# Transposing x and x1 by block flips and on-chip DMAs in a two-layer graph attention kernel

## The reference

```
layer 0:  q, k, v = x Wq', x Wk', x Wv' + bv          (per graph, 12 heads)
          s = q k' / sqrt(384) + (adj + adj);  p = softmax(s), 0 for rows of s that are all 0
          x1 = layernorm(x + (p v) Wo' + bo)
layer 1:  q, k, v = x1 Wq + bq, x1 Wk + bk, x1 Wv + bv
          s = q k' / sqrt(32) + beta adj, masked where adj <= 0;  p = softmax(s)
          out = layernorm(x1 + p v)
```

## Time and profile before

| | |
|---|---|
| time, median of 3 runs | 2354.26 us (2352.67 to 2358.37) |
| the profiled execution | 2356.46 us, span 2354.6 us |
| TensorE busy in matmuls | 2139.2 us, 91% of the span |
| VectorE | 1879.1 us, 80% |
| ScalarE | 1891.4 us, 80% |
| GpSimd | 1555.8 us, 66% |
| DMA engines, share of the span | 48.7%, 299 MB |
| mean granted clock of TensorE | 0.98 of full speed |

### The profile page before, as it was taken

How to read it: one execution, slowest core, us unless ns; L and a number is a source line. 1 busy time by engine, 2 the same in 40 slices (tenths; PEclk the granted TensorE clock), 3 DMA queues, 4 the chain that set the end, 5 groups by cost and what they waited for, 6 DMA issues and landing times.

```text
span 2354.6 us, 86096 instructions
## 1 busy us (share of the span) xinstructions
PE 2139.2 (91%) x23808; PEld 1929.9 (82%) x23808; DVE 1879.1 (80%) x8451; ACT 1891.4 (80%) x7688; POOL 1555.8 (66%) x2188
## 2 busy tenths in 40 slices
PE   5899999999999999999999999999999999999863
PEld 5888888888888888888888888888888888888853
DVE  4588888888888888888888888888888888887763
ACT  5688888888888888888888888888888888887764
POOL 5666666676776676676676676676676676676642
PEclk9999999999999999999999999999999999999975
DMA  5255454454554554554544544545545445444433
GB/s 141 74 135 129 130 139 127 129 140 126 128 140 122 133 138 119 137 135 119 143 129 122 141 129 122 139 129 127 134 129 132 129 129 137 124 130 124 121 100 78
DMA packets 234654, 299.36 MB, mean 127 GB/s; under 512 B 26704, under 2 KB 226384, under 8 KB 234576
## 3 DMA queue, kind: packets, MB, share of 16 engines
q1 hardware_dynamic: 234576, 298.43, 48.7%
HBM read 46.67 MB, written 25.17 MB: 31 GB/s over the span
## 4 chain that ended last, share of the span: by engine, by line
ACT 25%; issue 21%; POOL 21%; PE 15%; DVE 13%; ACTq 2%; POOLq 1%; DVEq 1%; DMA 1%; SPq 0%
ACT prob L586 19%; DVE neg_s L697 6%; POOL flip L914 4%; POOL x_bo L879 4%; PE s_bank L415 4%; PE r_bank L365 3%; PE r_bank L366 3%; PE r_bank L367 3%; POOL adj L903 3%; POOL mask L900 2%; POOL y L924 2%; POOL rstd L863 2%; ACT k0T L547 2%; POOL bias L889 1%; ACT k1T L551 1%
## 5 line engine op out<-in xcount | busy, mean ns | idle before, releaser
L586 ACT ACTIVATE prob<-neg_s,neg_max 128x128 f32<-128x128 f32 x3072 | 1183.3, 390 | 206.8 <-DVE neg_max L697 205.4
L697 DVE CUSTOM_DVE_ANT_0 neg_s<-s_bank,bias 128x128 f32<-128x128 f32 x3072 | 670.3, 286 | 147.8 <-PE s_bank L415 117.5
L586 ACT ACTIVATION_READ_ACCUMULATOR prob<-neg_s,neg_max 128x1 f32 x3072 | 589.6, 192 | 0.0
L932 POOL TENSOR_TENSOR prob<-prob,inv_sum 128x512 f32<-128x512 f32 x384 | 388.9, 1041 | 23.1 <-DVE inv_sum L785 19.8
L365 PE MATMUL r_bank<-x1T_hi,w_hi 128*128 128x256 f32 x1152 | 358.6, 311 | 3.4 <-ACT k0T L547 2.1
L365 PE MATMUL r_bank<-xT_hi,w_hi 128*128 128x256 f32 x1152 | 351.6, 305 | 10.5 <-DVE xT_lo L719 10.5
L914 POOL TENSOR_TENSOR flip<-neg_s 128x768 f32<-128x768 f32 x128 | 234.6, 1833 | 189.1 <-DVE neg_max L697 165.7
L367 PE MATMUL r_bank<-xT_hi,w_lo 128*128 128x256 f32 x1152 | 327.3, 284 | 0.0
L366 PE MATMUL r_bank<-x1T_lo,w_hi 128*128 128x256 f32 x1152 | 326.4, 283 | 0.0
L366 PE MATMUL r_bank<-xT_lo,w_hi 128*128 128x256 f32 x1152 | 326.3, 283 | 0.0
L367 PE MATMUL r_bank<-x1T_hi,w_lo 128*128 128x256 f32 x1152 | 325.4, 282 | 0.0
(11 more groups left out here) (75 smaller groups left out, 5424.2 us busy)
## 6 DMA issues: line engine op xcount, KB each, us to landing
prob0T<-flip SPq DMA_DIRECT2D x512, 192.0 KB, 3.5
prob1T<-stage SPq DMA_DIRECT2D x512, 192.0 KB, 3.7
x_in<-in_x_dram SPq DMA_DIRECT2D x128, 192.0 KB, 3.0
x_late<-x SPq DMA_DIRECT2D x64, 384.0 KB, 2.6
out_dram<-y SPq DMA_DIRECT2D x128, 192.0 KB, 2.3
adj<-in_adj_dram SPq DMA_DIRECT2D x256, 64.0 KB, 2.3
stage<-in_L_gnn_Wv_dram SPq DMA_DIRECT2D x2, 576.0 KB, 5.1
stage<-in_L_gnn_Wq_dram SPq DMA_DIRECT2D x2, 576.0 KB, 5.9
```

The lines of the kernel that those rows point to most:

```text
L586: act.activation(prob[layer][:, h, :], neg_s[layer][:, h, :], ACT.Exp, bias=neg_max[layer][:, h:h + 1], scale=-1.0, accum_out=row_sum[laye ...
L697: dve.tensor_tensor_reduce(neg_s[layer][:, h, :], s_bank[b][:, (h // HC) * N:(h // HC + 1) * N], bias[layer][q.parity][:, g, :], -1.0, BIG ...
L932: pool.tensor_tensor(prob[0][:, hs, :], prob[0][:, hs, :], inv_sum0[:, hs].unsqueeze(2).to_broadcast([P, HC, N]), ALU.mult).then_inc(probn ...
```

## The change

TensorE no longer transposes x and x1. `flip_xT` and `flip_x1T` on VectorE flip the 32x32 blocks of one graph's x or x1 into `flip_x`, `spread_rows` on SP moves the blocks between partitions with four DMAs for both graphs of a pair into `spread_x`, ScalarE copies the high part from there (`high_rows`), and GpSimd takes the low part (`low_rows`). x and x1 share `flip_x` and `spread_x`. The features come out in another order on the partitions, so the weights are loaded with their rows in that order, by three DMAs each.

x of pair n+2 is flipped near the end of body n and spread right behind the layer-0 probabilities of graph 1; its high part is still taken at the same place of the body of n+1. There is one more body at the start. x1 of pair n-1 is flipped in the middle of body n. The first eight users of the old ring (four of them transposes) go to a ring without the transposes; the Q and K product 4 of layer 0 and the scores of layer 1 go ahead of product 0 of layer 1 in TensorE's and ScalarE's queues. x, adj for layer 0 and the biases have one buffer each, so their loads and sums wait for the pair before. The layer-1 bias is made in two halves, and the second half goes to the end of the body.

```diff
-FIRST, LAST = -1, PAIRS + 3
+FIRST, LAST = -2, PAIRS + 3
...
-        x_in = [sb(f"x_in{b}", [P, 2, D]) for b in range(2)]
+        x_in = sb("x_in", [P, 2, D])
...
-        adj0 = [sb(f"adj0_{b}", [P, 2, N]) for b in range(2)]
+        adj0 = sb("adj0", [P, 2, N])
...
-        bias = [[sb(f"bias{l}_{b}", [P, 2, N]) for b in range(2)] for l in range(2)]
+        bias = [sb(f"bias{l}", [P, 2, N]) for l in range(2)]
...
+        flip_x = sb("flip_x", [P, NB, C, 2, HD])
+        spread_x = sb("spread_x", [P, NB, C, 2, HD])
...
+            def spread_rows(flipped, loaded, q):
+
+                if q.valid():
+                    sp.wait_ge(flipped, q.count(1, 1, 1))
+                    for i in range(NB):
+                        sp.dma_start(spread_x[:, i, :, :, :].rearrange("p c g b -> p (c g b)"),
+                                     flip_x[HD * i:HD * (i + 1), :, :, :, :].rearrange("p j c g b -> p (j c g b)")
+                                     ).then_inc(loaded, 16)
+
             def body(r, off):
                 n = Pair(r, off)
+                load_adj1(n.plus(-2))
                 store(n.plus(-4), 1)
                 keep_x1(n.plus(-2))
                 spread_probs(0, n, 0)
+                spread_rows(x1flip_done, x1t_loaded, n.plus(-1))
                 spread_probs(1, n.plus(-3), 1)
-                load_x(n.plus(3))
-                load_adj0(n.plus(3))
-                load_adj1(n.plus(-1))
+                if not is_peeled(r, off, -2):
+                    load_x(n.plus(2))
+                    load_adj0(n.plus(2))
                 store(n.plus(-3), 0)
                 spread_probs(0, n, 1)
+                spread_rows(xflip_done, xt_loaded, n.plus(2))
...
                 spread_probs(1, n.plus(-2), 0)
...
                 scores(0, n, 0, r)
-                transpose_x(nxt, 0, r)
-                transpose_x(nxt, 1, r)
...
-                transpose_x1(prev, 0, r)
-                transpose_x1(prev, 1, r)
...
+            def high_rows(dst, loaded, layer, done, q, g):
+                if q.valid():
+                    act.wait_ge(loaded, q.count(16 * NB // 2, 1, 16 * NB // 2))
+                    if g == 0:
+                        act.wait_ge(g_done[layer], q.count(3, 0, 0))
+                        act.wait_ge(v_done[layer], q.count(1, 0, 0))
+                    act.activation(dst[:, :, g * N:(g + 1) * N].rearrange("p c (i b) -> p c i b", i=NB),
+                                   spread_x[:, :, :, g, :].rearrange("p i c b -> p c i b"), ACT.Copy
+                                   ).then_inc(done, 1)
...
+                exps(0, n, 1, 2, 6)
                 high_x1T(prev, 0)
                 high_x1T(prev, 1)
...
-                exps(0, n, 1, 2, 9)
+                exps(0, n, 1, 6, 9)
...
+            def flip_rows(src, done, q, g):
+                dve.transpose(flip_x[:, :, :, g, :].rearrange("p j c b -> p c j b"),
+                              src.rearrange("p (c j a) -> p c j a", c=C, j=NB)).then_inc(done, 1)
...
                 flip_probs(0, n, 0)
+                attention_out1(prev3, 0)
+                flip_x1T(prev, 0)
                 inverse_sums1(prev3, 1)
                 flip_probs(1, prev3, 1)
-                attention_out1(prev3, 0)
+                flip_x1T(prev, 1)
                 values_out(0, nxt, 0)
...
                 flip_probs(0, n, 1)
+                flip_xT(nxt.plus(1), 0)
+                flip_xT(nxt.plus(1), 1)
+                attention_out1(prev3, 1)
                 inverse_sums1(prev2, 0)
                 flip_probs(1, prev2, 0)
...
+            def low_rows(dst, hi, hi_done, done, q, g):
+                if q.valid():
+                    m = slice(g * N, (g + 1) * N)
+                    pool.wait_ge(hi_done, q.count(1, g, 1))
+                    pool.tensor_tensor(dst[:, :, m].rearrange("p c (i b) -> p c i b", i=NB),
+                                       spread_x[:, :, :, g, :].rearrange("p i c b -> p c i b"),
+                                       hi[:, :, m].bitcast(F32).rearrange("p c (i b) -> p c i b", i=NB), ALU.subtract
+                                       ).then_inc(done, 1)
...
                 fold_scores0(n, 0)
                 inverse_std(1, prev4, 1)
+                low_xT(nxt, 0)
+                low_xT(nxt, 1)
                 normalise0(n, 0)
                 inverse_std(0, prev, 1)
-                make_bias1(prev2)
...
                 residual1(prev3, 0)
-
+                make_bias1(prev2, 0)
                 residual0(nxt, r)
-                make_bias0(nxt)
+
+                make_bias0(nxt, 0)
+                low_x1T(prev, 0)
+                low_x1T(prev, 1)
+                make_bias0(nxt, 1)
                 fold_scores0(n, 1)
                 inverse_std(1, prev3, 0)
                 normalise0(n, 1)
...
+                make_bias1(prev2, 1)
                 residual1(prev3, 1)
```

More of the change, by code:

```diff
@@ L275, in load_weights @@
                     sp.wait_ge(w_lo_done[i - NS], 1)
-                sp.dma_start(w_stage[i % NS], wts[i].rearrange("(c p) o -> p c o", p=P)
-                             ).then_inc(w_loaded[i], 16)
+                for c in range(C):
+                    rows = wts[i][c * P:(c + 1) * P, :]
+                    if i != WO0:
+                        rows = rows.rearrange("(j a) o -> a j o", j=NB)
+                    sp.dma_start(w_stage[i % NS][:, c, :], rows).then_inc(w_loaded[i], 16)
             load_x(Pair(0, 0))
@@ L486, in body @@
                 attend(0, n, 0, r)
+                project_qk(0, nxt, 4, r)
+                scores(1, prev2, 0, r)
                 project_qk(1, prev, 0, r)
-                scores(1, prev2, 0, r)
-                project_qk(0, nxt, 4, r)
                 project_out0(n, 0, r)
@@ L875, in residual0, with make_bias0 @@
                         pool.wait_ge(const_done, 1)
-                    pool.wait_ge(x_loaded[b], q.loads(2))
+                    pool.wait_ge(x_loaded, q.count(16, 1, 16))
                     pool.wait_ge(y0_done, q.plus(-2).count(1, 1, 1))
                     for g in range(2):
-                        pool.tensor_tensor(x_bo[b][:, g, :], x_in[b][:, g, :], bo_row[:], ALU.add
+                        pool.tensor_tensor(x_bo[b][:, g, :], x_in[:, g, :], bo_row[:], ALU.add
                                            ).then_inc(x_bo_done, 1)
-            def make_bias0(q):
+            def make_bias0(q, g):
@@ L884, in make_bias0 @@
                 if q.valid():
-                    b = q.parity
-                    pool.wait_ge(adj0_loaded[b], q.loads(2))
-                    pool.wait_ge(neg_done[0], q.plus(-2).count(H, 1, H))
-                    for g in range(2):
-                        pool.tensor_tensor(bias[0][b][:, g, :], adj0[b][:, g, :], adj0[b][:, g, :], ALU.add
-                                           ).then_inc(bias0_done, 1)
-            def make_bias1(q):
+                    pool.wait_ge(adj0_loaded, q.count(16, 1, 16))
@@ L894, in make_bias1 @@
+                    pool.wait_ge(neg_done[0], q.plus(-1).count(H, g, H))
+                    pool.tensor_tensor(bias[0][:, g, :], adj0[:, g, :], adj0[:, g, :], ALU.add
+                                       ).then_inc(bias0_done, 1)
+            def make_bias1(q, g):
                 if q.valid():
-                    b = q.parity
                     pool.wait_ge(adj1_loaded, q.count(16, 1, 16))
-                    pool.wait_ge(neg_done[1], q.plus(-2).count(H, 1, H))
+                    pool.wait_ge(neg_done[1], q.plus(-1).count(H, g, H))
+                    pool.wait_ge(bias1_steps, q.count(3, g, 0))
@@ L906, in make_bias1 @@
-                    for g in range(2):
-                        pool.tensor_tensor(bias[1][b][:, g, :], adj1[:, g, :], mask1[:, g, :], ALU.add).then_inc(bias1_steps, 1)
+                    pool.tensor_scalar(mask1[:], adj1[:, g, :], 0.0, -MASKED, ALU.is_le, ALU.mult
+                                       ).then_inc(bias1_steps, 1)
+                    pool.tensor_scalar(adj1[:, g, :], adj1[:, g, :], 0.0, beta_col[:], ALU.max, ALU.mult
+                                       ).then_inc(bias1_steps, 1)
@@ new lines, in make_bias1 @@
+                    pool.wait_ge(bias1_steps, q.count(3, g, 2))
+                    pool.tensor_tensor(bias[1][:, g, :], adj1[:, g, :], mask1[:], ALU.add).then_inc(bias1_steps, 1)
+            def low_rows(dst, hi, hi_done, done, q, g):
[6 more added lines that the diff above has]
+                                       ).then_inc(done, 1)
```

136 lines of the change are left out of this document (54 added, 82 removed).

## The result

The changed kernel takes 2746.16 us, median of 4 runs (2741.01 to 2747.39), beside 2354.37 us for the kernel before (median of 4): 1.166 times as long, 95% interval 1.1636 to 1.1678. The forecast was 2736 us. TensorE was rid of its transposes, and the whole got 392 us slower.

What follows compares the result with a forecast made beforehand. The bound was a 35.1 us loop through in-order queues, with TensorE nearly full. Both journeys make it 41.4: 2356.5 + 60 x 6.3 + 4 = 2738.5, less 2 for the median, 2736 us; range 2620 to 2920.

Steps and rivals of the forecast that it cites:

- Both journeys on one loop: The forecast: x's and x1's flip, spread and copies both lengthen the turn, 35.1 to 41.4 us; chance 0.74.
- the four terms: Graph-1 probability flip to exponentials behind x's copies 10.8 us, to normalisation 11.7, to graph-1 fold 10.4, to next flip 8.5.
- if ScalarE does not wait: Stated sign of a wrong prediction; ScalarE was to idle 2.5 to 3 us a turn before x's copies.
- The DMAs: SP's four spreading DMAs, for x and again for x1: 4.8 us from first issue to landing, bounds 4.2 and 6.05.
- The start: Before the first projection x must be flipped and spread, but weights arrive about then: 4 us once.
- a term of 6.3 us a turn: Predicted growth of one turn, 41.4 us against 35.1, charged for 60 turns.
- Single buffers and the bias half at nothing: Later loads of x and adj have over 8 us of cover; the bias half moved to the body's end: no cost.
- Rival, only x1's journey: x's spread lands before ScalarE asks; a loop through x1 and TensorE gives 37.5 us a turn, 2505 us; chance 0.06.
- Rival, the clock falls: TensorE's waits halve its clock once a turn, 1 to 2.5 us on the loop, 2800 to 2890 us; chance 0.10.
- What would show it: Profile signs: turn about 41 us, ScalarE idle before both copies, late fold, TensorE about 76%, first waiting at graph 1's value product.

Runs made afterwards that it cites:

- the two padded kernels: Changed kernel with four tiny DMAs on SP ahead of x's four spreading DMAs, or ahead of x1's: 2906.34 us and 2911.76 us.
- TensorE's delay filled away: Changed kernel with 12 matmuls, results thrown away, on TensorE ahead of its wait for layer 1's o1T of graph 1: 2738.60 us.
- three moves made: Changed kernel with graph 1's bias0 and fold ahead of x1's low parts, graph 0's bias1 ahead of the residual, x flipped and spread earlier: 2551.91 us.
- x early: Changed kernel with x's flips ahead of layer 1's negation and x's spread ahead of the graph-1 probabilities' DMAs: 2736.36 us.
- the slow stretch filled: Changed kernel with x's flips and spread moved earlier, plus 12 thrown-away matmuls ahead of TensorE's wait for o1T: 2663.53 us.
- one line of order: Graph 0's bias1 ahead of layer 1's residual: kernel before with single buffers 2484.60 to 2372.94 us; changed kernel with fold first 2618.33 to 2617.32.

## Why the prediction was right

*Both journeys on one loop.* Right, and shown by the two padded kernels: 2.8 and 2.7 us more a turn for 2.9 us of delay (2.5 and 2.6 by the medians). Three of the four terms held within 0.1 us in the mean, and the first was 0.4 us too long. But the prediction called itself wrong "if ScalarE does not wait", and in the second half of the run ScalarE doesn't wait for x's spread: the slow TensorE makes the scores as late as the spread. That this hardly changed the time is luck, for the sum has no such path. With TensorE's delay filled away, x's journey alone still sets 40.7 us a turn.

*The DMAs.* Four spreads with their landing were put at 4.8 us. For x it is 4.74 (1137.43 to the copy's start at 1142.17), for x1 4.26 (1116.83 to 1121.09), near the lower bound of 4.2; the medians over the middle turns in which the copy waited are 4.7 and 4.5. That is part of why the turn is 41.0 and not 41.4. The copies took 0.85 us as assumed (1142.17 to 1143.02), the subtractions 1.95 for two.

*The start.* Mis-sized: 4 us were charged, 16.9 came. The prediction counted only the flip and spread of the first x against the arrival of the weights. It missed that x of pair 1 has no buffer until GpSimd is done with pair 0: TensorE waits there 18.9 us for its low part. Earlier loading of it gave the start 3.8 us back (65.74, not 69.58); what makes the other 13 us was not tried. That the sum came close all the same is luck: a term of 6.3 us a turn that should have been 5.85 made this good, 60 x 6.3 + 4 = 382 beside 389 measured in the profile.

*Single buffers and the bias half at nothing.* In the changed kernel the half of the bias that stayed on the loop costs nothing, as far as its trace tells: GpSimd waits 2.06 us behind it for x1's copies. The prediction gave no such reason. What the single buffers cost in the changed kernel was not measured; in the start they are part of the 16.9 us, and with three moves made VectorE waits 1.1 us a turn for x's load. In the kernel before, the same edit costs 112 us. The prediction looked only at the half that moved to the end of the body, not at the half that stayed behind a waiting add.

*Rival, only x1's journey.* It did not come, and its number was too low. It took the way through TensorE at full clock and gave 37.5 us a turn. With x early the turn is 40.84, and 39.53 with the slow stretch filled; the change's second loop lies near 40 us. Even had this rival won, the time would have been some 2660 to 2740 us, not 2505.

*Rival, the clock falls.* It came in half: the clock falls once a turn, for about 3 us in the first half, as that rival had it, and for about 7 in the second. Yet it does not cost its 1 to 2.5 us a turn, because the exponentials that it delays are done 1 us before x's spread lands in the first half, and just as it lands in the second. Filled away, it is worth 8 us in the changed kernel.

*What would show it.* Seen: the turn of 41 us, TensorE at about 76% (80%, with the slow matmuls in it), GpSimd's wait for x1's copies and the fold behind them, VectorE's wait for the fold (2.72 us), and a DMA share of 49.6%. Not seen as told: ScalarE's pause ahead of x's copies shows only 0.98 us as the DMA's in the turn above and none in the second half, since 2.73 us of it, later 3.6, lie ahead of the first exponential, where the scores are late as well; the pause ahead of x1's copies is 0.80 us there and 1.2 in the mean, not 2; and TensorE's main wait is for o1T, not for the value product.

## What to carry to other kernels

When no engine is full, follow one loop through the queues and sum it stretch by stretch; here, work taken from the fullest engine was worth nothing, because it was handed to queues on that loop. Before costing an instruction at nothing, ask both what it waits behind and what stands behind it in its queue: one line of order was worth 112 us in one kernel and nothing in another. And keep the second-longest loop in the sum: it decides what every repair can bring, as x's early journey gave 10 us alone and 65 in company.

## What the runs showed of the hardware

Four DMAs of 96 KB from SBUF to SBUF took 4.26 us from the first issue to the waiting engine's start for x1 and 4.74 us for x in the turn shown (medians 4.5 and 4.7), both issued right behind four of 192 KB. SP issued four DMAs of 128 x 4 bytes in 2.78 us, no faster than four of 96 KB in the turns shown (2.49 to 2.84); four of 192 KB took it 3.08 and 3.14.

The granted clock fell from 2.4 to 1.2 GHz (1.00 to 0.50) once a turn, behind TensorE's pauses of 1.75 and 2.28 us, for about 3 us in 20 of the 48 turns from the eighth on and for about 7 us in 28, with the same two pauses ahead of it. With matmuls put into the second pause it fell in 33 of these turns, for about 3 us, and in those turns the added matmuls themselves ran slow, wholly or in part; with a pause of 0.57 us in that place it stayed at 1.00 there and fell behind a pause of 2.34 us at another.
